# The last block of an attention: its sums by TensorE and VectorE, its store in two parts

## The chip, the cores and the metric

The kernel runs on one core of a Trainium2 chip. The metric is the device time of one execution in microseconds (us), as the median of several runs. The core's engines are TensorE (PE; its weight loads are PEld), VectorE (DVE), ScalarE (ACT), GpSimd (POOL) and SyncE (SP), which here only issues transfers. Each engine works through its own list in order, and they wait for one another by semaphores.

## The reference, cut to what matters

Two images of 32 channels and 64 x 64 positions go through four layers, each added to its input; the last is an attention over all N = 4096 positions of an image.

```python
def _L3_conv_ref(x, w1, b1, w2, b2, w3, b3):
    xf = x.reshape(Bb, Cc, N)
    f1 = jnp.einsum('oc,bcn->bon', w1, xf) + b1[None, :, None]
    f2 = jnp.einsum('oc,bcn->bon', w2, xf) + b2[None, :, None]
    f3 = jnp.einsum('oc,bcn->bon', w3, xf) + b3[None, :, None]
    A = jax.nn.softmax(jnp.einsum('bcn,bcm->bnm', f1, f2), axis=-1)
    out = jnp.einsum('bcm,bnm->bcn', f3, A) + xf
    return out.reshape(Bb, Cc, Hh, Ww)
...
x = x + _L0_conv_ref(_gn(x), ...)
x = x + _L1_conv_ref(_gn(x), ...)
x = x + _L2_conv_ref(_gn(x), ...)
x = x + _L3_conv_ref(_gn(x), ...)
return x
```

## The kernel before

The attention is done one image after the other, each in eight blocks (`NBLK`) of 512 queries (`BLK`). Within a block a loop `s` goes over eight groups (`KEY_QUADS`) of four tiles of 128 keys. For each `s`:

- TensorE makes the scores of four key tiles, one to a PSUM bank (the banks `SCORES` to `SCORES + 3`), with a second, short product of three rows that subtracts each query's maximum;
- ScalarE takes the exponential of two banks at a time into `probs` (128 keys by 4 x 512 queries, two buffers); `probs_ready` counts the halves;
- TensorE multiplies the probabilities of the group before with the values `f3`. For image 1 (`weigh_values`) the four key tiles go to four column groups of 32, so the bank `SUMS` collects four partial numerators of 32 channels on its 128 partitions;
- for image 1, GpSimd adds the two halves of the probabilities (`add_pair`, 128x1024, into `pair_probs`), and TensorE multiplies the sum with ones (`weigh_ones`): the four column groups take 128 queries each, and the bank `SAMPLES` collects two halves of the softmax's totals, each 128 columns wide.

When a block of image 1 ends, its sums are finished beside the next block. ScalarE copies three pieces out of PSUM (`copy_sums`: `att_halves` and `halves_of_totals`). GpSimd adds the totals (`sum_part` with k = 0) and the numerators' upper and lower 64 partitions (k = 1). VectorE inverts the totals (`invert_totals`). ScalarE moves the second 32 rows of the numerators, and one row out of each of four groups of the inverses, onto image 1's partitions (`move_parts`: `lower_sum`, `inverse_row`). GpSimd adds the two rows of numerators (k = 2), multiplies by the inverse (k = 3) and adds the residual into `x_of[1]` (k = 4). After the last block the same steps run with nothing beside them. For image 0 other code does this on VectorE.

SyncE waits for the semaphore `x_final`, which counts finished blocks of both images, and stores each image whole: 32 partitions of 4096 numbers, 512 KB.

`stack` is a column of three 32x32 identities, used in an earlier layer to add three groups of 32 partitions by one product; VectorE makes it near 275 us by copies from `ident`. The pairs of lines that matter most, at the end of GpSimd's and of VectorE's program:

```python
for k in range(5):
    sum_part((0, 0, NBLK - 1), k, beside=False)
...
invert_totals((0, 0, NBLK - 1))
v.wait_ge(x_final, NBLK * B)
```

Of the kernel before, what the change touches and what calls it, by code (L numbers as in the profile page):

```python
# [67 lines left out]
def build(nc, x, off_w, off_b, conv_w, gamma, beta, l1_w, l1_ax, l1_aw, off2_w, off2_b, conv2_w, conv2_b,  # L68
# [10 lines left out]
    with ctx:  # L79
# [50 lines left out]
        stack = sb("stack", [3 * C, C])  # L130
# [61 lines left out]
        packed_values = scratch[:, 6 * BLK:8 * BLK].rearrange("p (m n) -> p m n", n=P)  # L192
        att_halves = scratch[0:2 * C, 4 * BLK:6 * BLK].rearrange("p (h n) -> p h n", h=2)
# [73 lines left out]
        x_final = sem("x_final"); pairs_added = sem("pairs_added"); parts_moved = sem("sum_parts_moved"); pool_sums = sem("pool_sums")  # L267
# [143 lines left out]
        def _(sp):  # L411
# [77 lines left out]
            for b in range(B):  # L489
                sp.wait_ge(x_final, NBLK * (b + 1))  # L490
                sp.dma_start(out[b].rearrange("c h w -> c (h w)"), x_of[b]).then_inc(out_stored, 16)
            sp.wait_ge(out_stored, 16 * B)

        @block.gpsimd
        def _(pool):
# [147 lines left out]
            def sum_part(j, k, beside=True):  # L643

                if 0 < k < 5 and beside:
                    pool.wait_ge(pairs_added, lin(j, KEY_QUADS, KEY_QUADS + k + 1))
                num, quotient = att_sum[IMAGE[1], 1, :], att_sum[IMAGE[1], 2, :]
                if k == 0:
                    pool.wait_ge(sums_copied, lin(j, 1, NBLK + 1))
                    pool.tensor_tensor(totals, halves_of_totals[:, 0:P], halves_of_totals[:, P:], ALU.add).then_inc(pool_sums, 1)  # L650
                elif k == 1:
                    pool.wait_ge(pool_sums, lin(j, POOL_SUMS, 1))
                    pool.tensor_tensor(att_sum[:, 0, :], att_halves[:, 0, :], att_halves[:, 1, :], ALU.add).then_inc(pool_sums, 1)
                elif k == 2:
                    pool.wait_ge(parts_moved, lin(j, 1, 1))
                    pool.tensor_tensor(num, att_sum[IMAGE[1], 0, :], lower_sum, ALU.add).then_inc(pool_sums, 1)
                elif k == 3:
                    pool.wait_ge(pool_sums, lin(j, POOL_SUMS, 3))
                    pool.tensor_tensor(quotient, num, inverse_row, ALU.mult).then_inc(pool_sums, 1)
                elif k == 4:  # L660
                    pool.wait_ge(pool_sums, lin(j, POOL_SUMS, 4))
                    at = lin(j, BLK)
                    here = slice(at, at + BLK) if isinstance(at, int) else bass.ds(at, BLK)
                    pool.tensor_tensor(x_of[1][:, here], x_of[1][:, here], quotient, ALU.add).then_inc(x_final, 1)

            def await_sum_part(j, k):
# [3 lines left out]
                elif k == 4:  # L670
                    pool.wait_ge(x_final, lin(j, 1, NBLK + 1))

            def second_attention():
# [9 lines left out]
                for s in range(KEY_QUADS):  # L683
# [3 lines left out]
                for k in range(5):  # L687
                    sum_part((0, 0, NBLK - 1), k, beside=False)
# [4 lines left out]
        def _(v):  # L693
# [307 lines left out]
            def place_bands():  # L1001
# [22 lines left out]
                for q in range(3):  # L1024
# [218 lines left out]

            def sum_part(b, j, k):
# [63 lines left out]
            def attention(b):  # L1308
# [10 lines left out]
                else:  # L1319
# [6 lines left out]
                    invert_totals((0, 0, NBLK - 1))  # L1326
                    v.wait_ge(x_final, NBLK * B)
# [70 lines left out]
        def _(act):  # L1398
# [284 lines left out]
            def attention(b):  # L1683
# [7 lines left out]
                else:  # L1691
# [7 lines left out]
                    copy_sums(b, (0, 0, NBLK - 1))  # L1699
                    move_parts((0, 0, NBLK - 1))  # L1700
# [50 lines left out]
        def _(pe):  # L1751
# [190 lines left out]
            def add_parts(i):  # L1942
# [5 lines left out]
                pe.matmul(psum[0:C, ADDED_BANK, 0:w], stack[:, :], conv_parts[:, 0:w], start=True, stop=True).then_inc(parts_added, 1)  # L1948
# [127 lines left out]

            def weigh(b, j, s, half):
# [74 lines left out]
            def attention(b):  # L2152
# [7 lines left out]
                else:  # L2160
# [7 lines left out]
                    weigh_values((0, 0, NBLK - 1), KEY_QUADS - 1)  # L2168
                    weigh_ones((0, 0, NBLK - 1), KEY_QUADS - 1)
# [72 lines left out]
```

## Time and profile before

| | before |
|---|---|
| median of three runs | 1275.58 us |
| lowest and highest of them | 1274.82 and 1275.71 us |
| the profiled execution, its own time | 1271.83 us |
| its span, from the first instruction to the last | 1270.0 us |
| busy in the span: PE, DVE, ACT, POOL | 1147.7, 956.1, 677.8, 684.8 us |
| mean granted TensorE clock, as a share of full speed | 0.948 |

The span is what the views of the trace cover; the execution's own time holds it and what lies around it. The profiled execution is one execution, and is not among the three runs. Busy times are sums over the whole span. They say little on the last 20 us, where one engine works at a time.

### The profile page before, as it was taken

How to read it: one execution, taken by the hardware profiler on the slowest of the kernel's cores; microseconds unless marked ns; L12 is line 12 of the kernel's file. 1: busy time of each engine (PE TensorE's matmuls, PEld its weight loads, DVE VectorE, ACT ScalarE, POOL GpSimd, SP SyncE). 2: the span in 40 equal slices, each digit the busy share in tenths (PEclk: the TensorE clock that was granted, in tenths of full speed). 3: DMA queues.
4: the chain of work that ended last, by engine and by line, in shares of the span. 5: the costliest groups of instructions: out<-in, count | busy, mean ns of one | idle time of the engine just before them, and what ended most of it. 6: DMA issues, size and time to landing. Idle time of an engine off the chain costs nothing.

```text
span 1270.0 us, 21675 instructions
## 1 busy us (share of the span) xinstructions
PE 1147.7 (90%) x7638; PEld 488.2 (38%) x7638; DVE 956.1 (75%) x1631; ACT 677.8 (53%) x930; POOL 684.8 (54%) x641
## 2 busy tenths in 40 slices
PE   4999997688999999979898898889899999999994
PEld 1788885154544443423332322232222222222221
DVE  6699998875766666668878888888768777777740
ACT  4876775756454555322244443443754466666663
POOL 7000000027777777777777777776000367777776
PEclk9999998698999999965699999999999899999998
DMA  2656550048454442111111111111000000000000
GB/s 55 143 130 122 114 118 1 1 141 253 138 145 128 149 143 70 52 48 50 52 53 52 50 52 51 50 52 48 1 1 1 1 18 1 0 1 0 1 1 17
DMA packets 59675, 79.26 MB, mean 62 GB/s; under 512 B 12230, under 2 KB 43974, under 8 KB 59414
## 3 DMA queue, kind: packets, MB, share of 16 engines
q1 hardware_dynamic: 44342, 47.03, 14.5%
q0 software_dynamic: 15264, 31.29, 8.7%
q8 instruction: 46, 0.75, 0.2%
q14 instruction: 23, 0.19, 0.1%
HBM read 70.94 MB, written 7.34 MB: 62 GB/s over the span
## 4 chain that ended last, share of the span: by engine, by line
PE 40%; POOL 34%; issue 14%; DVE 6%; ACT 3%; SPq 1%; DMA 1%; POOLq 0%; DVEq 0%; ACTq 0%
POOL tile_data L565 33%; PE psum L2107 6%; PE psum L2048 6%; PE psum L1813 6%; PE psum L2064 4%; PE psum L1828 3%; PE psum L2084 3%; DVE maxes L1215 2%; PE psum L1840 2%; PE psum L1763 2%; PE psum L2073 1%; PE psum L2113 1%; PE psum L2011 1%; PE psum L1831 1%; ACT quads L1667 1%
## 5 line engine op out<-in xcount | busy, mean ns | idle before, releaser
L565 POOL DMA_INDIRECT tile_data<-quad_table,index_u x477 | 467.0, 979 | 389.5 <-DMA quad_table<-quad_rows_or_splits 244.4
L1215 DVE TENSOR_REDUCE maxes<-psum 128x1 f32<-128x512 f32 x512 | 326.2, 683 | 90.4 <-PE psum L2048 89.0
L1667 ACT ACTIVATE quads<-psum 128x1024 f32<-128x1024 f32 x256 | 248.1, 1021 | 222.0 <-PE psum L2113 221.3
L640 POOL TENSOR_TENSOR tile_data<-quads 128x1024 f32<-128x1024 f32 x64 | 150.5, 2351 | 177.8 <-ACT quads L1667 132.4
L1928 PE MATMUL psum<-scratch,quad_rows_or_splits 128*128 128x512 f32 (+1 forms) x486 | 211.5, 577 | 6.7 <-DVE scratch L1037 6.7
L2107 PE MATMUL psum<-quads,probs_and_weighted 32*128 32x512 f32 x1024 | 147.2, 644 | 2.5 <-ACT quads L1667 2.4
L2084 PE MATMUL psum<-quads 128*64 128x512 f32 x512 | 131.2, 617 | 0.0
L1928 PEld LDWEIGHTS psum<-scratch,quad_rows_or_splits 128*128 128x128 f32 x486 | 88.6, 193 | 104.0 <-issue 88.7
L2048 PE MATMUL psum<-products_or_attention 128*128 128x512 bf16 x256 | 90.5, 416 | 37.0 <-DVE maxes L1215 37.0
L1049 DVE TENSOR_TENSOR probs_and_weighted<-psum,quads 128x512 f32<-128x512 f32 (+1 forms) x81 | 51.4, 642 | 75.9 <-PE psum L1928 70.7
L1512 ACT ACTIVATE vals<-psum 96x384 f32<-96x384 f32 x53 | 25.8, 486 | 142.8 <-PE psum L1892 142.8
L2048 PE MATMUL psum<-quad_rows_or_splits,tile_data 128*128 128x512 bf16 x256 | 82.6, 389 | 5.3 <-DVE maxes L1215 3.6
L1813 PE MATMUL psum<-quad_rows_or_splits 64*128 64x128 f32 x1152 | 81.4, 283 | 1.5 <-DVE in_reach L817 1.5
L1542 ACT ACTIVATE quads<-quads,band_columns 128x512 f32<-128x512 f32 (+1 forms) x81 | 49.6, 676 | 54.8 <-DVE probs_and_weighted L1049 54.8
L2048 PEld LDWEIGHTS psum<-products_or_attention 128*128 (+1 forms) x256 | 19.9, 98 | 149.2 <-DVE maxes L1215 106.3
L1813 PEld LDWEIGHTS psum<-quad_rows_or_splits 64*128 64x128 f32 x1152 | 69.3, 187 | 12.4 <-issue 6.3
L2064 PE MATMUL psum<-quads 128*32 128x512 f32 x512 | 68.2, 605 | 0.8 <-ACT quads L1667 0.7
L952 DVE TENSOR_TENSOR probs_and_weighted<-tile_data,psum 128x1152 f32<-128x1152 f32 x45 | 60.6, 1346 | 0.3
L831 DVE TENSOR_TENSOR probs_and_weighted<-psum,tile_data 128x384 f32<-128x384 f32 x96 | 52.8, 550 | 7.0 <-DVE sampled L850 5.1
L1763 PE MATMUL psum<-quads,off_w 128*32 128x512 f32 x256 | 32.8, 659 | 27.5 <-DMA w_sb<-in_b 17.8
L2107 PEld LDWEIGHTS psum<-quads,probs_and_weighted 32*128 32x128 f32 x1024 | 40.4, 184 | 44.8 <-issue 22.2
L1037 DVE SCALAR_TENSOR_TENSOR scratch<-products_or_attention,band_columns,psum 128x512 f32<-128x512 f32 (+1 forms) x81 | 51.8, 692 | 5.2 <-ACT psum L1547 5.2
(241 smaller groups left out, 1578.7 us busy)
## 6 DMA issues: line engine op xcount, KB each, us to landing
products_or_attention<-positions SPq DMA_DIRECT2D x30, 576.0 KB, 8.4
products_or_attention<-bands SPq DMA_DIRECT2D x12, 768.0 KB, 7.3
tile_data<-quad_table,index_u POOLq DMA_INDIRECT x477, 2.5
quads<-bands SPq DMA_DIRECT2D x6, 768.0 KB, 10.5
quad_table<-quad_rows_or_splits SPq DMA_DIRECT2D x4, 768.0 KB, 8.3
products_or_attention<-bands SPq DMA_DIRECT2D x4, 576.0 KB, 8.5
quad_table<-quad_rows_or_splits SPq DMA_DIRECT2D x2, 640.0 KB, 8.4
products_or_attention<-positions SPq DMA_DIRECT2D x4, 288.0 KB, 6.9
```

Of the source, the lines that this page charges most:

```text
L565: pool.indirect_dma_start(out=out[:, k * CORNERS * C:(k + 1) * CORNERS * C], out_offset=None, in_=table, in_offset=bass.IndirectOffsetOnAx ...
L640: pool.tensor_tensor(pair_probs[:, s % 2, :], probs[:, s % 2, 0:2 * BLK], probs[:, s % 2, 2 * BLK:4 * BLK], ALU.add)\
L952: v.tensor_tensor(weighted[:, :].rearrange("p (q k c) -> p k q c", q=CORNERS, c=C), corners_of.rearrange("p (k q c) -> p k q c", k=TAPS, q ...
L1215: v.reduce_max(maxes[:, tile_of_q, block_of_k:block_of_k + 1], psum[:, FREE + c % 2, :], AXIS_X)\
L1667: act.activation(probs[:, s % 2, 2 * BLK * h:2 * BLK * (h + 1)], psum[:, SCORES + 2 * h:SCORES + 2 * h + 2, :].rearrange("p a n -> p (a n) ...
L1763: pe.matmul(psum[C * g:C * g + C, bank, :].rearrange("p (y x) -> p y x", x=W), off_w_sb[d][:, s, :], grid[:, y:y + 8, sx:sx + W], start=s ...
L1813: last = pe.matmul(psum[:, mix_bank(b, ky), P * kx:P * kx + P], hat_x[rows, n % 2, 3 * ky + kx, :], img_t[rows, (2 * n + ky) * C:(2 * n + ...
L1928: last = pe.matmul(psum[:, m, 0:width(n)], band_img[:, j, 4 * C * m:4 * C * (m + 1)], band_sel[:, n % 2, j, 0:width(n)], start=j == 0, sto ...
L2048: pe.matmul(psum[:, FREE + c % 2, :], qa[b][:, tile_of_q], ka[b][:, lo:lo + BLK], start=True, stop=True).then_inc(chunk_scored, 1)
L2064: pe.matmul(psum[C * i:C * i + C, SUMS, :], f3[1][:, 4 * s + i, 0:C], probs[:, s % 2, BLK * i:BLK * i + BLK], start=s == 0, stop=s == KEY_ ...
L2084: last = pe.matmul(psum[2 * C * h:2 * C * h + 2 * C, SUMS, :], f3[b][:, 4 * s + i, :], probs[:, s % 2, BLK * i:BLK * i + BLK], start=s == ...
L2107: pe.matmul(psum[:, SCORES + i, :], keys[b][mine, P * s:P * s + P], q_now[mine, :], start=True, stop=False)
```

## The change

For the last block of image 1 alone, the sums are finished in another way.

- TensorE multiplies both halves of the last group's probabilities with ones itself (two products of four column groups in place of one on the halves' sum), each before the half's values product. GpSimd's last pair sum and its five last `sum_part` steps go.
- VectorE takes the two halves of the totals from PSUM, adds and inverts them (`last_sums`).
- TensorE spreads the inverses: four products with a row of ones, one for each group of 128 queries, from partitions 0, 32, 64 and 96 into four banks, all onto image 1's 32 partitions. ScalarE copies these into `inverse_row`.
- ScalarE copies the whole bank `SUMS` into `last_block`; TensorE adds its four groups of 32 partitions by one product with `stack`, which has a fourth identity now.
- VectorE multiplies that sum by `inverse_row`, out of PSUM, and adds the residual.
- Finished blocks of image 1 count in a semaphore of their own, `second_final`. Image 1 is stored in two parts: seven blocks (448 KB) when the seventh is finished, and the last block (64 KB) when that is.

```diff
-        stack = sb("stack", [3 * C, C])
+        stack = sb("stack", [P, C])
...
+        last_block = scratch[:, 6 * BLK:7 * BLK]
...
-            for b in range(B):
-                sp.wait_ge(x_final, NBLK * (b + 1))
-                sp.dma_start(out[b].rearrange("c h w -> c (h w)"), x_of[b]).then_inc(out_stored, 16)
-            sp.wait_ge(out_stored, 16 * B)
+            sp.wait_ge(x_final, NBLK)
+            sp.dma_start(out[0].rearrange("c h w -> c (h w)"), x_of[0]).then_inc(out_stored, 16)
+            for blocks, here in ((NBLK - 1, slice(0, N - BLK)), (NBLK, slice(N - BLK, N))):
+                sp.wait_ge(second_final, blocks)
+                sp.dma_start(out[1].rearrange("c h w -> c (h w)")[:, here], x_of[1][:, here]).then_inc(out_stored, 16)
+            sp.wait_ge(out_stored, 48)
...
-                for s in range(KEY_QUADS):
+                for s in range(KEY_QUADS - 1):
                     await_sum_part((0, 0, NBLK - 2), s - 1)
                     add_pair((0, 0, NBLK - 1), s, ahead=False)
                     sum_part((0, 0, NBLK - 2), s)
-                for k in range(5):
-                    sum_part((0, 0, NBLK - 1), k, beside=False)
...
-                for q in range(3):
+                for q in range(4):
                     mine = slice(C * q, C * q + C)
                     last = v.tensor_copy(stack[mine, :], ident[mine, mine])
...
+            def last_sums():
+
+                here = slice(N - BLK, N)
+                quotient = att_sum[IMAGE[1], 2, :]
+                v.wait_ge(last_products, 1)
+                v.wait_ge(second_final, NBLK - 1)
+                v.tensor_copy(halves_of_totals[:, 0:P], psum[:, SAMPLES, 0:P]).then_inc(last_steps, 1)
+                v.wait_ge(last_steps, 1)
+                v.tensor_tensor(totals, psum[:, SAMPLES, P:2 * P], halves_of_totals[:, 0:P], ALU.add).then_inc(last_steps, 1)
+                v.wait_ge(last_steps, 2)
+                v.reciprocal(inverses, totals).then_inc(last_steps, 1)
+                v.wait_ge(last_products, 4)
+                v.wait_ge(last_moved, 2)
+                v.tensor_tensor(quotient, psum[IMAGE[1], FREE + 1, :], inverse_row, ALU.mult).then_inc(last_steps, 1)
+                v.wait_ge(last_steps, 4)
+                v.tensor_tensor(x_of[1][:, here], x_of[1][:, here], quotient, ALU.add).then_inc(second_final, 1)
...
-                    invert_totals((0, 0, NBLK - 1))
-                    v.wait_ge(x_final, NBLK * B)
+                    last_sums()
...
-                    copy_sums(b, (0, 0, NBLK - 1))
-                    move_parts((0, 0, NBLK - 1))
+                    act.wait_ge(last_products, 2)
+                    act.activation(last_block, psum[:, SUMS, :], ACT.Identity).then_inc(last_moved, 1)
+                    act.wait_ge(last_products, 3)
+                    act.wait_ge(second_final, NBLK - 1)
+                    act.activation(inverse_row.rearrange("p (g n) -> p g n", g=4), psum[IMAGE[1], SCORES:SCORES + 4, 0:P], ACT.Identity).then_inc(last_moved, 1)
...
+            def end_last_block():
+
+                s, last = KEY_QUADS - 1, 2 * KEY_QUADS * NBLK * B
+                for half in range(2):
+                    pe.wait_ge(probs_ready, last - 1 + half)
+                    if half == 0:
+                        pe.wait_ge(summed, KEY_QUADS * NBLK * B - 1)
+                    by_query = probs[:, s % 2, 2 * BLK * half:2 * BLK * (half + 1)].rearrange("p (h n) -> p h n", h=2)
+                    for g in range(4):
+                        ones_done = pe.matmul(psum[C * g:C * g + C, SAMPLES, 0:2 * P].rearrange("p (h n) -> p h n", h=2), ones[:, 0:C],
+                                              by_query[:, :, P * g:P * g + P], start=False, stop=half == 1)
+                    if half:
+                        ones_done.then_inc(last_products, 1)
+                    for i in (2 * half, 2 * half + 1):
+                        done = pe.matmul(psum[C * i:C * i + C, SUMS, :], f3[1][:, 4 * s + i, 0:C],
+                                         probs[:, s % 2, BLK * i:BLK * i + BLK], start=False, stop=True)
+                done.then_inc(last_products, 1)
+                pe.wait_ge(last_steps, 3)
+                for g in range(4):
+                    done = pe.matmul(psum[IMAGE[1], SCORES + g, 0:P], ones[C * g:C * g + 1, 0:C], inverses[C * g:C * g + 1, :],
+                                     start=True, stop=True)
+                done.then_inc(last_products, 1)
+                pe.wait_ge(last_moved, 1)
+                pe.matmul(psum[IMAGE[1], FREE + 1, :], stack[:, :], last_block, start=True, stop=True).then_inc(last_products, 1)
...
-                    weigh_values((0, 0, NBLK - 1), KEY_QUADS - 1)
-                    weigh_ones((0, 0, NBLK - 1), KEY_QUADS - 1)
+                    end_last_block()
```

How this stands in the engines' lists is shown at three places. The rows give the line, the operation, output and inputs, the output's shape, and what an instruction waits for. The names are those of the memory that holds a buffer: `quads` holds `probs` and `f3`; `tile_data` holds `pair_probs`, the totals and the inverses; `scratch` holds the numerators and `last_block`.

TensorE, from the last scores of image 1 to its program's end, before:

```order
L2107 MATMUL psum<-quads,probs_and_weighted 128x512 [waits probs_ready]
...
L2064 MATMUL psum<-quads 32x512 [waits probs_ready]
L2064 MATMUL psum<-quads 32x512 x3
L2073 MATMUL psum<-tile_data,ones 32x256 [waits pairs_added]
L2073 MATMUL psum<-tile_data,ones 32x256 x3
L79 UNCONDITIONAL_BRANCH
```

and with the change, from the seventh group's ones product on:

```order
L2094 MATMUL psum<-tile_data,ones 32x256 x3
L2107 MATMUL psum<-quads,ones 32x256 [waits sums_done,probs_ready]
L2107 MATMUL psum<-quads,ones 32x256 x3
L2112 MATMUL psum<-quads 32x512 x2
L2107 MATMUL psum<-quads,ones 32x256 [waits probs_ready]
L2107 MATMUL psum<-quads,ones 32x256 x3
L2112 MATMUL psum<-quads 32x512 x2
L2117 MATMUL psum<-tile_data,ones 32x128 [waits last_steps]
L2117 MATMUL psum<-tile_data,ones 32x128 x3
L2121 MATMUL psum<-scratch,stack 32x512 [waits last_sums_moved]
L79 UNCONDITIONAL_BRANCH
```

The last wait for GpSimd (`pairs_added`) is gone; two ones products stand ahead of the halves of the values product, and five products on the sums themselves follow, behind waits for VectorE and ScalarE.

VectorE, from the last step on the maxima to its program's end (line 1242 of before is line 1244 of the changed program); before:

```order
L1236 TENSOR_TENSOR nm_parts<-neg_max,nm_parts 128x16 [waits nm_steps]
L1242 RECIPROCAL tile_data<-tile_data 128x128 [waits pool_sums] x2
L79 UNCONDITIONAL_BRANCH [waits x_final]
```

and with the change:

```order
L1244 RECIPROCAL tile_data<-tile_data 128x128 [waits pool_sums]
L1252 COPY tile_data<-psum 128x128 [waits second_image_final,last_products]
L1254 TENSOR_TENSOR tile_data<-psum,tile_data 128x128 [waits last_steps]
L1256 RECIPROCAL tile_data<-tile_data 128x128 [waits last_steps]
L1259 TENSOR_TENSOR scratch<-psum,tile_data 32x512 [waits last_sums_moved,last_products]
L1261 TENSOR_TENSOR x_state<-x_state,scratch 32x512 [waits last_steps]
```

One inverse that waited for GpSimd's totals becomes five operations that wait for TensorE, for ScalarE and for VectorE itself.

GpSimd, from the residual of the seventh block to its program's end, before:

```order
L664 TENSOR_TENSOR x_state<-x_state,scratch 32x512 [waits pool_sums,pairs_added]
L640 TENSOR_TENSOR tile_data<-quads 128x1024 [waits sums_done,probs_ready,x_final]
L640 TENSOR_TENSOR tile_data<-quads 128x1024 [waits sums_done,probs_ready] x2
L650 TENSOR_TENSOR tile_data<-tile_data 128x128 [waits sums_copied]
L653 TENSOR_TENSOR scratch<-scratch 64x512 [waits pool_sums]
L656 TENSOR_TENSOR scratch<-scratch,tile_data 32x512 [waits sum_parts_moved]
L659 TENSOR_TENSOR scratch<-scratch,tile_data 32x512 [waits pool_sums]
L664 TENSOR_TENSOR x_state<-x_state,scratch 32x512 [waits pool_sums]
L79 UNCONDITIONAL_BRANCH
```

and with the change:

```order
L668 TENSOR_TENSOR x_state<-x_state,scratch 32x512 [waits pool_sums,pairs_added]
L644 TENSOR_TENSOR tile_data<-quads 128x1024 [waits sums_done,probs_ready,second_image_final]
L644 TENSOR_TENSOR tile_data<-quads 128x1024 [waits sums_done,probs_ready]
L79 UNCONDITIONAL_BRANCH
```

GpSimd ends with the pair sum of the seventh group; six operations behind it are gone. The rest of all five lists is in the same order as before, apart from the fourth copy into `stack` on VectorE, the three stores at the end of SyncE's list, and ScalarE's two copies in place of eight.

## Rows read from the trace of the kernel before

**Rows 1.** The page's first line: the profiled execution's span.
```profile
span 1270.0 us, 21675 instructions
```

**Rows 2.** Chain that ended last, its end: start us, us, engine and line.
```profile
1253.35 2.36 POOL tile_data L640
...
1264.43 1.29 POOLq L79
```

**Rows 3.** Timeline of the end: start us, us, engine, line, operation, count, idle before.
```profile
1245.57 1.26 POOL L664 TENSOR_TENSOR x_state<-x_state,scratch 32x512 f32<-32x512 f32 x1
...
1251.34 1.94 ACT L1667 ACTIVATE quads<-psum 128x1024 f32<-128x1024 f32 x2 [1.80 <-PE psum L2113]
...
1252.06 0.61 PE L2073 MATMUL psum<-tile_data,ones 128*32 128x256 f32 x8
...
1255.76 0.64 PE L2073 MATMUL psum<-tile_data,ones 128*32 128x256 f32 x8 [1.36 <-POOL tile_data L640]
1256.46 0.59 ACT L1639 ACTIVATE scratch<-psum 64x512 f32<-64x512 f32 x1 [3.19 <-PE psum L2073]
...
1258.13 0.45 POOL L650 TENSOR_TENSOR tile_data<-tile_data 128x128 f32<-128x128 f32 x1 [2.43 <-ACT tile_data L1642]
1258.62 0.95 DVE L1242 RECIPROCAL tile_data<-tile_data 128x128 f32<-128x128 f32 x1 [26.55 <-POOL tile_data L650]
...
1259.95 0.63 ACT L1648 ACTIVATE tile_data<-scratch 32x512 f32<-32x512 f32 x1 [1.90 <-POOL scratch L653]
...
1264.47 1.25 POOL L664 TENSOR_TENSOR x_state<-x_state,scratch 32x512 f32<-32x512 f32 x1
1265.75 0.34 SPq L491 DMA_DIRECT2D out_x<-x_state  x1
```

**Rows 4.** DMA issues: tensors, queue, count, KB each, median us to landing.
```profile
positions<-scratch SPq DMA_DIRECT2D x4, 256.0 KB, 2.0
out_x<-x_state SPq DMA_DIRECT2D x2, 512.0 KB, 3.9
```

**Rows 5.** Windows around both stores: stretch, its length, busy, PEclk, DMA share, GB/s.
```profile
25.40:26.30 0.90, 0.90 (x12) 0.24 (x8) 0.90 (x1) 0.90 (x1) 0.75 (x2) 1.00 0.77 291
...
1265.75:1266.55 0.80, 0.00 (x0) 0.00 (x0) 0.00 (x0) 0.00 (x0) 0.00 (x0) 0.50 0.00 0
1266.55:1269.25 2.70, 0.00 (x0) 0.00 (x0) 0.00 (x0) 0.00 (x0) 0.00 (x0) 0.50 0.92 194
```

**Rows 6.** Timeline, four places: products of the new shapes' nearest kinds on TensorE.
```profile
546.01 1.04 PE L1948 MATMUL psum<-scratch,stack 96*32 96x512 f32 x2 [0.70 <-ACT scratch L1556]
...
700.40 0.84 PE L1900 MATMUL psum<-vals,conv_w 96*32 96x128 f32 x6
...
703.00 1.94 PE L2084 MATMUL psum<-quads 128*64 128x512 f32 x8
...
1249.89 1.14 PE L2107 MATMUL psum<-quads,probs_and_weighted 32*128 32x512 f32 x8
```

**Rows 7.** Groups by line and shape on VectorE: busy us, mean ns, idle before.
```profile
L1049 DVE TENSOR_TENSOR probs_and_weighted<-psum,quads 128x512 f32<-128x512 f32 x54 | 37.1, 688 | 59.2 <-PE psum L1928 55.9 <-PE psum L1938 3.4
L1049 DVE TENSOR_TENSOR probs_and_weighted<-psum,quads 128x384 f32<-128x384 f32 x27 | 14.4, 550 | 16.6 <-PE psum L1928 14.8 <-PE psum L1938 1.8
L1266 DVE TENSOR_TENSOR x_state<-x_state,scratch 32x512 f32 x5 | 3.4, 680 | 0.0
```

**Rows 8.** Timeline: VectorE's next operation behind the copies into `stack`.
```profile
277.67 0.46 DVE L739 COPY scratch<-psum 128x288 f32<-128x288 f32 x1 [2.43 <-PE psum L1871]
```

**Rows 9.** Windows at the end, as in rows 5.
```profile
1253.00:1257.00 4.00, 1.70 (x16) 0.32 (x16) 0.00 (x0) 0.81 (x2) 2.35 (x1) 1.00 0.00 0
1257.00:1260.00 3.00, 0.00 (x0) 0.00 (x0) 0.95 (x1) 1.08 (x4) 1.71 (x2) 1.00 0.00 0
1260.00:1270.00 10.00, 0.00 (x0) 0.00 (x0) 0.00 (x0) 1.70 (x5) 3.76 (x3) 0.51 0.25 52
```

**Rows 10.** DMA queues of 1230 to 1270 us: packets, MB, share of 16 engines.
```profile
q8 instruction: 2, 0.03, 0.4%
```

More of the change, by code:

```diff
@@ L266, in build @@
         sums_copied = sem("sums_copied"); sum_steps = sem("sum_steps"); residuals = sem("residuals_added")
-        x_final = sem("x_final"); pairs_added = sem("pairs_added"); parts_moved = sem("sum_parts_moved"); pool_sums = sem("pool_sums")
+        x_final = sem("x_final"); second_final = sem("second_image_final")
+        last_products = sem("last_products"); last_moved = sem("last_sums_moved"); last_steps = sem("last_steps"); pairs_added = sem("pairs_added"); parts_moved = sem("sum_parts_moved"); pool_sums = sem("pool_sums")
         block = ctx.enter_context(nc.Block())
@@ L641, in add_pair, with sum_part @@
                     .then_inc(pairs_added, 1)
-            def sum_part(j, k, beside=True):
-                if 0 < k < 5 and beside:
+            def sum_part(j, k):
+                if 0 < k < 5:
                     pool.wait_ge(pairs_added, lin(j, KEY_QUADS, KEY_QUADS + k + 1))
@@ L663, in sum_part @@
                     here = slice(at, at + BLK) if isinstance(at, int) else bass.ds(at, BLK)
-                    pool.tensor_tensor(x_of[1][:, here], x_of[1][:, here], quotient, ALU.add).then_inc(x_final, 1)
+                    pool.tensor_tensor(x_of[1][:, here], x_of[1][:, here], quotient, ALU.add).then_inc(second_final, 1)
             def await_sum_part(j, k):
@@ L670, in await_sum_part @@
                 elif k == 4:
-                    pool.wait_ge(x_final, lin(j, 1, NBLK + 1))
+                    pool.wait_ge(second_final, lin(j, 1, 1))
             def second_attention():
@@ L1947, in add_parts @@
                 w = width(TAPS * i)
-                pe.matmul(psum[0:C, ADDED_BANK, 0:w], stack[:, :], conv_parts[:, 0:w], start=True, stop=True).then_inc(parts_added, 1)
+                pe.matmul(psum[0:C, ADDED_BANK, 0:w], stack[0:3 * C, :], conv_parts[:, 0:w], start=True, stop=True).then_inc(parts_added, 1)
             def dense_and_tiles():
```

## Prediction

> **What bounds the kernel now.** I read the page first, for the span: 1270.0 us [rows 1]; the profiled execution took 1271.83 us as a whole, so 1.83 us lie around the span, and the median of the runs, 1275.58 us, is 3.75 us above that execution. I work out the change of the span, and carry it unchanged to the median.
>
> The change touches only what comes after the last block's scores, so the view that matters is the chain of waits at its end [rows 2]: after VectorE's and TensorE's work in the blocks, the last pieces, five of them, are all POOL's, from the pair sum at 1253.35 to 1264.43 and its program's end, with the residual in it. The timeline of that stretch [rows 3] shows why: from the end of the seventh ones product (1252.06 + 0.61 = 1252.67) to the issue of image 1's store at 1265.75 the engines take turns, each waiting for the one ahead. The second exponential of the last group of keys ends at 1251.34 + 1.94 = 1253.28; POOL's pair sum holds the last ones product back until 1255.76; ScalarE moves three pieces from 1256.46; POOL adds the totals from 1258.13, VectorE inverts them in 0.95, POOL adds the parts, ScalarE moves five pieces from 1259.95 on, and POOL does three more operations, the last in 1.25 from 1264.47, until 1265.72. Nothing else is in progress, so each microsecond taken out here is one of the span. The store then lands 3.9 us after its issue [rows 4]. Cut into stretches [rows 5], this is 0.80 us without a byte, 2.70 us of transfer at 194 GB/s, and about 0.4 us more to the landing.
>
> **The change, part by part.** *Removed from the chain:* POOL's last pair sum and its five operations, ScalarE's eight small activations, VectorE's old inverse. The path from 1252.67 to 1265.75, 13.08 us, is replaced.
>
> *Added:* I follow the new path from 1252.67. For each hand-over between engines I take 0.05 us: the rows show 0.06 from TensorE to ScalarE (1255.76 + 0.64 = 1256.40, then 1256.46) and 0.04 from POOL to VectorE (1258.13 + 0.45 = 1258.58, then 1258.62) [rows 3]; I take the same where VectorE waits for itself.
> 1. TensorE starts on the first half of the last probabilities 0.06 after 1252.67, since they are there by then (the second half too, at 1253.28). A ones product over four column groups with 256 columns took 0.64 [rows 3]. There are two instead of one, since the halves are no longer added first. Half of a values product uses two of four column groups; the nearest row is image 0's, with two groups and 512 columns, two halves in 1.94, so 0.97 each [rows 6]. Up to the end of the second ones product: 0.64 + 0.97 + 0.64 = 2.25. The other half of the values (0.97) and ScalarE's copy of the sums (0.59, as at 1256.46) end at about 1256.6, while VectorE works.
> 2. VectorE copies half the totals out of PSUM, adds the other half, inverts. With a PSUM operand it took 688 ns for 512 columns and 550 for 384 [rows 7], 138 less per 128 columns, so 0.27 for 128; I take 0.29, and 0.95 for the inverse: 1.53.
> 3. TensorE spreads the inverses: four products of one row by 128 columns, on four row groups, into four banks. This is not in the trace. One after the other, as three accumulating products of 128 columns took 0.84 [rows 6], it would be 1.12. Side by side, 0.35 at least: one such product is 0.28. The row of the scores, four row groups into four banks, took 1.14 for 512 columns, hardly more than the 1.04 of a single product of 512 columns [rows 6], so row groups do run side by side here; I take 0.45.
> 4. TensorE adds the four column groups by one product with four stacked identities: 1.04, the row of the same product with three [rows 6]. ScalarE's copy of the spread inverses (0.63) is hidden under it.
> 5. VectorE multiplies (0.69, a PSUM operand) and adds the residual (0.68) [rows 7]; then SP issues the store, 0.03 later as now.
>
> Work 2.25 + 1.53 + 0.45 + 1.04 + 1.37 = 6.64; hand-overs 0.06 at the start, six of 0.05, 0.03 at the end: 0.39. The store is issued at 1252.67 + 7.03 = 1259.70, 6.05 earlier.
>
> *The store:* 64 KB in runs of 2 KB instead of 512 KB. The store of positions, 256 KB, landed in 2.0 [rows 4], moving at 291 GB/s [rows 5]; 64 KB take 0.23 at that rate. With 0.80 ahead and 0.3 to 0.4 behind, 1.45; 2.0 is the upper bound, since four times the bytes need no more. Gain 2.45. The rows split that duration into a part which no smaller store loses (1.1 to 1.2) and one that goes with the bytes.
> The Trainium skill, page "DMA: Bandwidth & Descriptors", section "Anatomy of one DMA — SWDGE (gpsimd) path", gives about 2.0 us fixed and 436 GB/s for the rest. By that the small store would take an estimated 2.15, the gain here would be 1.75 and the sum 7.80 instead of 8.50. The trace does not bear it out: the same rule gives 2.6 for the 256 KB that landed in 2.0.
>
> *Moved:* the other 448 KB are issued when block 6 is final, at 1245.57 + 1.26 = 1246.83 [rows 3], and even at the 3.9 us of the whole store have landed some 10 us before the new end; SP has nothing else queued. They run beside block 7, whose POOL operations are on the path; I price that at nothing, as the transfers go to DMA engines that carried nothing there, and at 0.5 at most for two pair sums.
>
> *The fourth identity block* costs VectorE one more 32x32 copy, about 0.17, near 275 us. Behind the copies VectorE waits 2.43 us for TensorE [rows 8], which covers it; bare, it would be 0.2 us.
>
> Sum: 6.05 + 2.45 = 8.50. Span 1261.5, profiled execution 1263.3, median 1267.1.
>
> **The rivals.**
> *The store is no faster when small.* Its time would be a wait for the memory, not the bytes: 3.9 stays, gain 6.05, time 1269.5. For it: the parts before and behind the transfer are constant. Against it: 256 KB in 2.0 and a transfer of 2.70 in the middle of this very store.
> *TensorE's tail is slow.* The granted clock is full (2.4 GHz) over 1253 to 1257 and 1257 to 1260, though TensorE did nothing in the latter; over 1260 to 1270 it is 0.51 [rows 9], half (1.2 GHz) for nearly all of it. If it fell before 1257, steps 3 and 4 would cost 1.49 more; with step 3 one by one, 0.67 more. Time 1267.8 to 1269.3. Against it: the new path keeps TensorE busy to about 1256 and again until 1258, where now it stops at 1256.40.
> *Nothing to measure.* About 0.2%, 2.6 us, is what a measurement of this kernel can tell from no change. The gain would have to shrink by 6 us over seven hand-overs, 0.9 each where the rows show 0.04 to 0.08. Time around 1274.
> *Slower.* Code is fetched by DMA: two packets of the instruction queue in the last 40 us, at 0.4% of sixteen engines' time 1.28 us each [rows 10]. The additional copy near 275 us moves all later code of VectorE, loops included, by one instruction. If a border of what is fetched then fell into a loop, each pass could wait about 1.3 us; from nine such passes (2.6 + 8.5 = 11.1 us) the kernel is slower, with sixteen about 1279. Against it: in the rows of the end no engine waits for code, although such a packet lies among them.
>
> **How the numbers follow.** The forecast has 0.78, the unshortened store 0.08, a slow TensorE 0.07, nothing 0.03, slower 0.04. Within the forecast: step 3 up to 0.67 more or 0.10 less; the store up to 0.55 more; the early part of the store up to 0.5; step 1 about 0.3 less if its pieces overlap. That is 1266.5 to 1268.9, and the runs of before spread over 0.9, so 1266.0 to 1269.3; taking in the rivals that still gain 6 us or more, 1265.3 to 1270.0. Faster by over 0.2%: 0.78 + 0.08 + 0.07 = 0.93; within it 0.03; slower 0.04.
>
> **What would show it.** Right: the timeline of after has the first half's ones product right behind the seventh one's end; VectorE's three small operations in about 1.6; the spreads in under 0.5 with starts close together; the stack product in about 1.04 at full clock; the store issued some 7.0 us after the seventh ones product, and landed about 1.5 after its issue. Wrong: spreads 0.28 apart, a stack product of 2 us, a second store that lands after 2 us or more, VectorE's operations with waits of half a microsecond between them, or a block 7 longer than now while the first part of the store moves.

## The result, and the profile after

The changed kernel took 1265.89 us (median of four runs, 1263.46 to 1266.97) against 1275.20 for before (four runs, 1274.17 to 1275.71). The ratio is 0.9932, with a 95% interval of 0.9917 to 0.9946. The forecast was 1267.1, a ratio of 0.9933. The measured median lies inside the forecast's wide range (1265.3 to 1270.0) and 0.1 us below its narrower one (1266.0 to 1269.3). The profiled execution took 1263.46 us over a span of 1261.7; before it was 1270.0 [rows 1].

The timeline of the changed kernel's end, in the columns of [rows 3], from the residual of block 6 (the seventh, counted from 0) over the seventh ones product, from whose end both kernels' tails are measured, to the issue of the last store (weight loads and some products are left out; L668 is the residual, L2094 the seventh ones product, L2107 are ones products, L2112 values, L2117 spreads, L2121 the stack product):

```profile
1245.85 1.26 POOL L668 TENSOR_TENSOR x_state<-x_state,scratch 32x512 f32<-32x512 f32 x1
...
1252.34 0.61 PE L2094 MATMUL psum<-tile_data,ones 128*32 128x256 f32 x8
...
1253.13 0.64 PE L2107 MATMUL psum<-quads,ones 128*32 128x256 f32 x8 [0.18 <-PE psum L2094]
...
1253.56 0.62 PE L2112 MATMUL psum<-quads 128*32 128x512 f32 x2
1253.62 0.62 PE L2107 MATMUL psum<-quads,ones 128*32 128x256 f32 x4
...
1254.63 0.41 PE L2107 MATMUL psum<-quads,ones 128*32 128x256 f32 x2
1255.12 0.29 DVE L1252 COPY tile_data<-psum 128x128 f32<-128x128 f32 x1 [22.76 <-PE psum L2112]
1255.18 0.60 ACT L1718 ACTIVATE scratch<-psum 128x512 f32<-128x512 f32 x1 [1.63 <-PE psum L2112]
1255.44 0.29 DVE L1254 TENSOR_TENSOR tile_data<-psum,tile_data 128x128 f32<-128x128 f32 x1
1255.77 0.95 DVE L1256 RECIPROCAL tile_data<-tile_data 128x128 f32<-128x128 f32 x1
...
1256.78 0.42 PE L2117 MATMUL psum<-tile_data,ones 1*32 1x128 f32 x8 [1.68 <-DVE tile_data L1256]
...
1257.13 1.06 PE L2121 MATMUL psum<-scratch,stack 128*32 128x512 f32 x2
1257.26 0.59 ACT L1721 ACTIVATE tile_data<-psum 32x512 f32<-32x512 f32 x1 [1.49 <-PE psum L2117]
1258.22 0.68 DVE L1259 TENSOR_TENSOR scratch<-psum,tile_data 32x512 f32<-32x512 f32 x1 [1.50 <-PE psum L2121]
1258.94 0.68 DVE L1261 TENSOR_TENSOR x_state<-x_state,scratch 32x512 f32<-32x512 f32 x1
...
1259.65 0.31 SPq L495 DMA_DIRECT2D out_x<-x_state  x1
```

The seventh ones product ends at 1252.95 here (1252.67 before), the last store is issued at 1259.65: 6.70 us instead of 13.08. Two things are to be seen besides. Values products (from 1253.56) and ones products (from 1253.62) run beside one another, and the last ones product ends at 1254.63 + 0.41 = 1255.04. VectorE's copy at 1255.12 waits, by the program, for that last ones product; the row puts its wait down to the values' line.

Image 1's two stores in the DMA issues of the changed kernel, as in [rows 4]:

```profile
out_x<-x_state SPq DMA_DIRECT2D x1, 448.0 KB, 3.5
out_x<-x_state SPq DMA_DIRECT2D x1, 64.0 KB, 1.6
```

The last store lands in 1.6 us instead of 3.9. The stretch from the seventh ones product to the last landing is so 6.70 + 1.6 = 8.30 instead of 13.08 + 3.9 = 16.98, 8.68 less. The spans differ by 8.3, mostly because the seventh ones product ended 0.28 later in this execution.

### The profile page after: what moved, and what is told of

The parts are those of the page before. It is cut to its first block, busy times and chain, and to the rows that moved or that the text cites. A ratio compares the mean times of both kernels' runs of the same rounds, so it can differ in the third digit from the quotient of the medians.

```text
span 1261.7 us, 21645 instructions
## 1 busy us (share of the span) xinstructions
PE 1139.2 (90%) x7595; PEld 490.1 (39%) x7656; DVE 958.5 (76%) x1636; ACT 675.6 (54%) x924; POOL 678.4 (54%) x635
## 4 chain that ended last, share of the span: by engine, by line
PE 48%; POOL 19%; DVE 14%; issue 12%; ACT 4%; SPq 1%; DMA 1%; DVEq 1%; POOLq 0%; ACTq 0%
POOL tile_data L569 19%; PE psum L2153 8%; PE psum L2069 8%; PE psum L1834 6%; PE psum L2130 5%; DVE maxes L1217 5%; PE psum L2085 4%; PE psum L1849 3%; DVE probs_and_weighted L954 3%; PE psum L1784 2%; PE psum L1861 2%; PE psum L2159 2%; DVE probs_and_weighted L964 2%; PE psum L2094 1%; PE psum L2032 1%
## 5 line engine op out<-in xcount | busy, mean ns | idle before, releaser
L2069 PE MATMUL psum<-products_or_attention 128*128 128x512 bf16 x226 | 83.2, 416 | 42.7 <-DVE maxes L1217 37.6
L2069 PE MATMUL psum<-quad_rows_or_splits,tile_data 128*128 128x512 bf16 x225 | 75.1, 387 | 9.7 <-issue 4.9
```

Source lines behind the costliest of these rows:

```text
L2069: pe.matmul(psum[:, FREE + c % 2, :], qa[b][:, tile_of_q], ka[b][:, lo:lo + BLK], start=True, stop=True).then_inc(chunk_scored, 1)
```

## The experiments

Single executions of one kernel lie some microseconds apart, and the runs here scatter more than those shown first: in the first group before took 1269.87 to 1276.04 in 27 runs, median 1272.77, in the second 1269.15 to 1275.89 in 17, median 1274.18. For steps of one or two microseconds the verdict therefore rests on two stretches of the timeline, each from one profiled execution: from the seventh ones product's end to the last store's issue, and from there to its landing (read to 0.1 us). The first four experiments belong to the first group, the others to the second; the changed kernel was not run in the second, so comparisons with it there go by the stretches.

**The store alone.** The kernel before, with this edit:

```diff
-            for b in range(B):
-                sp.wait_ge(x_final, NBLK * (b + 1))
-                sp.dma_start(out[b].rearrange("c h w -> c (h w)"), x_of[b]).then_inc(out_stored, 16)
+            sp.wait_ge(x_final, NBLK)
+            sp.dma_start(out[0].rearrange("c h w -> c (h w)"), x_of[0]).then_inc(out_stored, 16)
+            for blocks, here in ((2 * NBLK - 1, slice(0, N - BLK)), (2 * NBLK, slice(N - BLK, N))):
+                sp.wait_ge(x_final, blocks)
+                sp.dma_start(out[1].rearrange("c h w -> c (h w)")[:, here], x_of[1][:, here]).then_inc(out_stored, 16)
```

> The kernel before, with only image 1's store in two parts. My theory (the store's gain stands by itself, by the bytes it no longer moves at the end): the last store is issued 13.1 us after the seventh ones product as before, and lands 1.6 us after its issue instead of 3.9, so 2.3 us less, ratio 0.998. Rival A (all of the gain comes from the sums, the split only moves waiting about): within 0.3 us of before. Rival B (the 448 KB beside block 7 take time from GpSimd's pair sums): the gain shrinks to 1.8 us, with pair sums above 2.4 us in the timeline.

Its timeline and its DMA issue of the last store:

```profile
1244.18 1.26 POOL L666 TENSOR_TENSOR x_state<-x_state,scratch 32x512 f32<-32x512 f32 x1
...
1248.21 2.36 POOL L642 TENSOR_TENSOR tile_data<-quads 128x1024 f32<-128x1024 f32 x1 [0.34 <-ACT quads L1669]
...
1250.67 0.61 PE L2075 MATMUL psum<-tile_data,ones 128*32 128x256 f32 x8
...
1264.35 0.31 SPq L493 DMA_DIRECT2D out_x<-x_state  x1
```

```profile
out_x<-x_state SPq DMA_DIRECT2D x1, 64.0 KB, 1.6
```

From 1251.28 to 1264.35 it is 13.07 us, as before, and the store lands in 1.6: up to the landing, 2.3 us are the store's own, as my theory said. The pair sum beside the 448 KB takes 2.36, as elsewhere, and from the end of block 6's residual (1245.44) to the end of the seventh ones product it is 5.84 us, as in before (1246.83 to 1252.67): rival B falls. The ratio of the runs, 0.9992 (0.9980 to 1.0004), cannot tell the expected 0.998 from no change; by itself it leaves rival A open, and the timeline decides.

Not all of the 2.3 us reaches the end of the span in this execution. The span ends 15.62 us after the seventh ones product, against 17.33 in before: 1.7 less. Behind the landing SyncE waits for the end of TensorE's program, here longer than the 0.2 us of the other nine profiles (line, what it waited for, us in total, times, longest):

```profile
SPq L79 <- PEq L79: 0.7, 1, 0.7
```

Why is not known, and one execution does not show whether it returns. What the short store is worth on top of the new sums is seen without it in the next experiment and the changed kernel run once more, in the same group: medians of 1267.00 and 1264.52, and spans that end 10.95 and 8.70 us after the seventh ones product, 2.25 us apart.

**The sums alone.** The changed kernel, image 1 stored whole:

```diff
-            for blocks, here in ((NBLK - 1, slice(0, N - BLK)), (NBLK, slice(N - BLK, N))):
-                sp.wait_ge(second_final, blocks)
-                sp.dma_start(out[1].rearrange("c h w -> c (h w)")[:, here], x_of[1][:, here]).then_inc(out_stored, 16)
+            sp.wait_ge(second_final, NBLK)
+            sp.dma_start(out[1].rearrange("c h w -> c (h w)"), x_of[1]).then_inc(out_stored, 16)
...
```

> The changed kernel, with image 1 stored whole at the end. My theory: the store is issued 6.7 us after the seventh ones product, as in the changed kernel, and lands 3.9 to 4.0 us after its issue; 6.4 us less than before, 2.3 us more than the changed kernel, ratio 0.995. Rival A (all of the gain comes from the sums): 8.7 us less than before.

```profile
1251.84 0.61 PE L2093 MATMUL psum<-tile_data,ones 128*32 128x256 f32 x8
...
1259.14 0.34 SPq L494 DMA_DIRECT2D out_x<-x_state  x1
```

These lines of its timeline give 1259.14 - 1252.45 = 6.69 us; the store of 512 KB lands in 3.9. The ratio is 0.9959 (0.9946 to 0.9972), so 3.6 to 6.9 us, which holds the 6.4 expected and excludes the 8.7 of rival A.

**TensorE's ones alone.** The kernel before without GpSimd's last pair sum; ones and values in the halves' order of the changed kernel, everything behind them as before:

```diff
-                for s in range(KEY_QUADS):
+                for s in range(KEY_QUADS - 1):
                     await_sum_part((0, 0, NBLK - 2), s - 1)
                     add_pair((0, 0, NBLK - 1), s, ahead=False)
...
+            def end_last_block():
...
-                    weigh_values((0, 0, NBLK - 1), KEY_QUADS - 1)
-                    weigh_ones((0, 0, NBLK - 1), KEY_QUADS - 1)
+                    end_last_block()
```

> The kernel before, with only GpSimd's last pair sum replaced by TensorE's two ones products on the halves; copies, totals, parts, quotient, residual and store as before. Theory 1 (the pieces of step 1 overlap over column groups, as the changed kernel's timeline suggests): sums are complete 2.15 us after the seventh ones product instead of 3.73, the store is issued 1.6 us earlier, ratio 0.9988. Theory 2 (the prediction's step 1, durations one after the other: 0.64 + 0.97 + 0.64 + 0.97 and the start): 3.3 us, so 0.4 us earlier. Both: the rest of the chain as long as before.

```profile
1253.18 0.61 PE L2073 MATMUL psum<-tile_data,ones 128*32 128x256 f32 x8
...
1256.00 0.59 ACT L1639 ACTIVATE scratch<-psum 64x512 f32<-64x512 f32 x1 [1.60 <-PE psum L2089]
...
1265.28 0.34 SPq L491 DMA_DIRECT2D out_x<-x_state  x1
```

ScalarE starts 2.21 us after the seventh ones product's end (1253.79), and the store is issued 11.49 after it, 1.59 earlier than before: theory 1, and not a sum of durations as in the prediction's step 1. The ratio, 0.9987 (0.9973 to 1.0001), agrees with 1.6 us, but does not exclude 0.4. So of the 6.4 us of the sums, 1.6 come from the pair sum and, by difference, 4.8 from what follows.

**The changed kernel once more.**

> The changed kernel once more, beside the others. My theory: 8.3 to 9.0 us less than before; the stretch from the seventh ones product's end to the store's issue 6.7 us, the landing 1.6 us. Rival (TensorE's granted clock falls early in some executions, since in the changed kernel's profile it fell at about 1258 us, in the stack product): the stack product takes up to 2.1 us and the stretch 7.7 us.

```profile
1255.29 0.61 PE L2094 MATMUL psum<-tile_data,ones 128*32 128x256 f32 x8
...
1260.09 1.04 PE L2121 MATMUL psum<-scratch,stack 128*32 128x512 f32 x2
...
1262.60 0.32 SPq L495 DMA_DIRECT2D out_x<-x_state  x1
```

1262.60 - 1255.90 = 6.70 again, the landing 1.6, the stack product 1.04 at full clock. The rival's early fall of the clock does not occur in this execution. The ratio is 0.9936 (0.9920 to 0.9952), 8.2 us less, just under the 8.3 to 9.0 expected, all of which the interval holds. Its span, though, is 1264.6, because the seventh ones product ends 3 us later than in the first profile.

**Ones first.** The changed kernel, the ones products of both halves ahead of the values:

```diff
                     for g in range(4):
                         ones_done = pe.matmul(psum[C * g:C * g + C, SAMPLES, 0:2 * P].rearrange("p (h n) -> p h n", h=2), ones[:, 0:C],
                                               by_query[:, :, P * g:P * g + P], start=False, stop=half == 1)
-                    if half:
-                        ones_done.then_inc(last_products, 1)
-                    for i in (2 * half, 2 * half + 1):
-                        done = pe.matmul(psum[C * i:C * i + C, SUMS, :], f3[1][:, 4 * s + i, 0:C],
-                                         probs[:, s % 2, BLK * i:BLK * i + BLK], start=False, stop=True)
+                ones_done.then_inc(last_products, 1)
+                for i in range(4):
+                    done = pe.matmul(psum[C * i:C * i + C, SUMS, :], f3[1][:, 4 * s + i, 0:C],
+                                     probs[:, s % 2, BLK * i:BLK * i + BLK], start=False, stop=True)
```

> The changed kernel, with both of TensorE's ones products on the halves ahead of all four values products. Times from the seventh ones product's end. My theory (the path that ends last goes by the totals; the values have about 1.2 us to spare): VectorE starts at 1.4 us instead of 2.2, the store is issued at 5.9 instead of 6.65, 0.75 us less than the changed kernel. Rival (the values and the stack product end last): VectorE's inverse is earlier, but the store's issue stays within 0.2 us of 6.65.

```profile
1251.47 0.61 PE L2094 MATMUL psum<-tile_data,ones 128*32 128x256 f32 x8
1252.27 1.11 PE L2107 MATMUL psum<-quads,ones 128*32 128x256 f32 x16 [0.18 <-PE psum L2094]
1253.19 1.04 PE L2111 MATMUL psum<-quads 128*32 128x512 f32 x8
1253.44 0.29 DVE L1252 COPY tile_data<-psum 128x128 f32<-128x128 f32 x1 [21.96 <-PE psum L2107]
...
1257.96 0.31 SPq L495 DMA_DIRECT2D out_x<-x_state  x1
```

VectorE starts 1.36 us after 1252.08, and the store is issued after 5.88, 0.82 earlier than in the changed kernel: the totals' path was the longer one. The values, moved behind the ones (L2111), still reach ScalarE in time. The two ones products, one right behind the other on the same four column groups, take 1.11 us and not twice 0.64. The ratio to before is 0.9920 (0.9904 to 0.9937).

**Inverses moved instead of spread.** The changed kernel without the four spreads; ScalarE and VectorE move two rows of inverses each:

```diff
-                pe.wait_ge(last_steps, 3)
-                for g in range(4):
-                    done = pe.matmul(psum[IMAGE[1], SCORES + g, 0:P], ones[C * g:C * g + 1, 0:C], inverses[C * g:C * g + 1, :],
-                                     start=True, stop=True)
-                done.then_inc(last_products, 1)
...
+                v.wait_ge(last_steps, 3)
+                for g in (2, 3):
+                    v.tensor_copy(inverse_row[:, P * g:P * g + P], inverses[C * g:C * g + C, :]).then_inc(last_steps, 1)
...
-                    act.activation(inverse_row.rearrange("p (g n) -> p g n", g=4), psum[IMAGE[1], SCORES:SCORES + 4, 0:P], ACT.Identity).then_inc(last_moved, 1)
+                    for g in range(2):
+                        last = act.activation(inverse_row[:, P * g:P * g + P], inverses[C * g:C * g + C, :], ACT.Identity)
+                    last.then_inc(last_moved, 1)
```

> The changed kernel without the four spreads on TensorE and without ScalarE's copy of them: ScalarE and VectorE move two of the four rows of inverses each, straight to the place where they are multiplied; the stack product no longer stands behind the spreads. My theory (the spreads cost not only their 0.42 us, but hold the stack product back until the inverse is there): the stack product runs from 2.9 to 3.95 us after the seventh ones product's end, beside the inverse, and the store is issued at 5.9 us instead of 6.65. Rival (moves on ScalarE and VectorE are slower than the spreads, as the 1.25 us for four of them before): 1.25 us from the inverse to the product, and no gain over the changed kernel.

```profile
1254.15 0.61 PE L2100 MATMUL psum<-tile_data,ones 128*32 128x256 f32 x8
...
1257.63 1.05 PE L2122 MATMUL psum<-scratch,stack 128*32 128x512 f32 x2 [0.73 <-ACT scratch L1722]
1258.56 0.63 ACT L1726 ACTIVATE tile_data<-tile_data 32x128 f32<-32x128 f32 x2 [0.98 <-DVE tile_data L1256]
1258.56 0.47 DVE L1259 COPY tile_data<-tile_data 32x128 f32<-32x128 f32 x2
1259.32 0.68 DVE L1263 TENSOR_TENSOR scratch<-psum,tile_data 32x512 f32<-32x512 f32 x1 [0.29 <-ACT tile_data L1726]
...
1260.75 0.32 SPq L495 DMA_DIRECT2D out_x<-x_state  x1
```

The stack product now runs beside the inverse (2.87 to 3.92 us after 1254.76), VectorE multiplies 0.71 earlier than in the changed kernel, and the store is issued at 5.99 instead of 6.70. Two moves on each engine take 0.63 and 0.47 side by side; the rival's 1.25 would have been four on one. The ratio is 0.9912 (0.9898 to 0.9927).

**Both of these edits.**

> The changed kernel with both: ones products ahead of the values, and inverses moved by ScalarE and VectorE. My theory: the inverse ends at 3.0 us after the seventh ones product's end, the moves at 3.7, and the stack product, behind the values and ScalarE's copy, at 3.95, so that it ends last; store issued at 5.4 us, 1.25 less than the changed kernel. Rival (the two gains add up): 5.15 us.

```profile
1255.36 0.61 PE L2100 MATMUL psum<-tile_data,ones 128*32 128x256 f32 x8
...
1258.84 1.04 PE L2121 MATMUL psum<-scratch,stack 128*32 128x512 f32 x2 [0.72 <-ACT scratch L1722]
1258.96 0.63 ACT L1726 ACTIVATE tile_data<-tile_data 32x128 f32<-32x128 f32 x2 [0.18 <-DVE tile_data L1256]
...
1259.97 0.68 DVE L1263 TENSOR_TENSOR scratch<-psum,tile_data 32x512 f32<-32x512 f32 x1 [0.54 <-PE psum L2121]
...
1261.40 0.31 SPq L495 DMA_DIRECT2D out_x<-x_state  x1
```

Issued 5.43 us after 1255.97: 1.27 less than the changed kernel, not the 1.53 of both gains added. VectorE's last wait (0.54) is for the stack product: the path through the values, ScalarE's copy and the stack product now ends last. The median, 1261.34, is the lowest of all; the ratio to before, 0.9899 (0.9884 to 0.9915), is 10.8 to 14.8 us, while the two stretches give 13.08 - 5.43 + 2.3 = 9.95. Why the runs show more than the stretches was not settled. The profiled execution, at 1265.22, is the slowest of the five by 3.7 us, and its seventh ones product ends latest of all ten profiles. Between these ten that end, which the edits do not touch, lies up to 4.7 us apart, more than the 2.9 between the medians' difference and the stretches.

**The fourth identity alone.** The kernel before with `range(4)` in place of `range(3)` at the copies into `stack`, and the larger `stack`:

> The kernel before, with only the fourth identity in the stack: one more copy on VectorE near 275 us, so that all of VectorE's later code stands one instruction further. My theory: no difference in the end's stretches (13.1 us from the seventh ones product to the store's issue, landing 3.9 us), and a time within 0.2% of before. Rival (the moved code makes loops wait for code): passes of VectorE's loops longer by about 1.3 us, 2.6 us or more in all.

The ratio is 0.9998 (0.9988 to 1.0008). No cost in VectorE's loops is seen; the interval leaves room for 1.0 us and excludes the rival's 2.6. The end's stretch, however, was 13.42 and not 13.1, by one product:

```profile
1253.58 0.61 PE L2073 MATMUL psum<-tile_data,ones 128*32 128x256 f32 x8
...
1257.27 1.01 PE L2073 MATMUL psum<-tile_data,ones 128*32 128x256 f32 x8 [1.36 <-POOL tile_data L640]
...
1267.61 0.34 SPq L491 DMA_DIRECT2D out_x<-x_state  x1
```

The last ones product took 1.01 us instead of 0.64. The windows of this execution say why; the last three columns are the granted clock, the DMA share and GB/s:

```profile
1253.50:1257.30 3.80, 1.79 (x24) 0.35 (x21) 0.00 (x0) 1.29 (x2) 2.35 (x1) 1.00 0.00 0
1257.40:1258.40 1.00, 0.88 (x8) 0.03 (x4) 0.00 (x0) 0.07 (x1) 0.00 (x0) 0.50 0.00 0
```

The clock had fallen to half (1.2 GHz) after a stretch in which TensorE was busy for 1.79 of 3.80 us. In the profile of before the same products, with TensorE busy for 1.70 of 4.00 us, were followed by full clock until about 1260 [rows 9]; so before's stretch is 13.1 us in two profiles and 13.4 in this one.

## Why the prediction was right, step by step

Forecast and measured, for the profile of the changed kernel:

| step | forecast us | measured us |
|---|---|---|
| start behind the seventh ones product | 0.06 | 0.18 |
| 1: to the second ones product's end | 2.25 | 1.91 |
| 2: hand-over, copy, add, inverse | 1.68 | 1.68 |
| 3: hand-over and spreads, to the stack product's start | 0.50 | 0.41 |
| 4: stack product | 1.04 | 1.06 |
| 5: hand-over, multiply, residual, issue | 1.50 | 1.46 |
| sum | 7.03 | 6.70 |
| landing of the last store | 1.45 | 1.6 |

- The mechanism and both parts of the gain were right, and up to the landing the parts add: 2.3 us by the store alone, 6.4 by the sums alone, 8.7 together. The medians of the runs give 0.9, 5.8 and 8.3, with intervals that hold 2.3, 6.4 and 8.7.
- That the ratio was met to 0.0001 is luck. Its interval is 1.9 us to either side, and the errors of the steps (+0.12, -0.34, -0.09, +0.02, -0.04, and +0.15 at the landing) cancel in part. By its own terms the narrower range should also have been 1266.2 to 1269.3: 1267.1 less 0.4 and plus 1.72 is 1266.7 to 1268.8, where the prediction has 1266.5 to 1268.9.
- Step 1 was mis-sized by 0.34. It added the durations of products that in the rows overlap: values at 1253.56 and ones at 1253.62, which the program puts on different column groups. The run with TensorE's ones alone has the same order and the same shorter time in another surrounding. Different groups are not all of it: two ones products on the same four groups also took 1.11 instead of 1.28 (ones first). The text had named this overlap as 0.3 in its range.
- The start was taken as 0.06, the hand-over from TensorE to ScalarE. Where TensorE waits for its own earlier product, the rows show 0.18.
- Step 3 had the widest bounds, 0.35 to 1.12. The four spreads took 0.42 for all eight records, where one after the other was put at 1.12, so the row groups work side by side here too. Within the sum that was right, but the larger cost of the spreads was not seen: they hold the stack product back until the inverse is there. Without them the kernel issues its store 0.71 earlier.
- The store landed in 1.6 us in all six profiles that have it, and image 1 stored whole in 3.9 in the other four; the forecast from this kernel's own stores was 1.45. In windows of 0.1 us the bytes move from 1260.45 to 1260.85, some 0.4 us, where the prediction took 0.23; the 0.8 ahead of them was right. By the figures of the Trainium skill's page "DMA: Bandwidth & Descriptors", section "Anatomy of one DMA — SWDGE (gpsimd) path", the estimate was 2.15, which this trace does not bear out; the page gives them for transfers on GpSimd's path, and this one is issued by SyncE.
- The early 448 KB cost block 7 nothing: from the end of block 6's residual to the end of the seventh ones product it is 5.84 us without them (before) and with them (1247.11 to 1252.95 here, and the same with the store alone). The fourth copy was covered as said: VectorE's wait behind it went from 2.43 [rows 8] to 2.23, in this line of the changed kernel's timeline:

```profile
278.63 0.46 DVE L741 COPY scratch<-psum 128x288 f32<-128x288 f32 x1 [2.23 <-PE psum L1892]
```

- Of the rivals, an unshortened store is ruled out by the landing, moved code by the run with the fourth identity alone. A slow TensorE was nearer than its 0.07 said: in the changed kernel's profile the clock fell between 1258.0 and 1258.1, with 0.1 to 0.2 us of the stack product left, as its windows show, and the product took 1.06 instead of 1.04. Had it fallen 1 us earlier, the product would by estimate have been 0.6 to 0.9 us longer: at half clock the ones product above went from 0.64 to 1.01, and image 0's values in before's profile from 1.94 [rows 6] to 3.68 (at 992.17 us).

```profile
1253.00:1258.00 5.00, 3.19 (x34) 1.27 (x34) 1.53 (x3) 1.73 (x3) 0.00 (x0) 1.00 0.02 3
1258.10:1259.00 0.90, 0.08 (x1) 0.00 (x0) 0.74 (x2) 0.00 (x0) 0.00 (x0) 0.50 0.00 0
```

## What to carry to other kernels

At the end of a kernel, where engines hand one small piece of work after another along, the pieces on the path that ends last are the price, and a piece taken off it brings its time, up to the point where another path ends last (both edits together gave 1.27 us here, not 1.53). Durations may only be added where the rows do not overlap. Count there, and store early whatever is final early, so that the last store is small. Then ask which of two paths ends last, and order the work for it: here the totals needed their products first, and a product that waited for the inverse stood ahead of one that did not. Steps of one or two microseconds are read from a stretch between two fixed points of the timeline, when single executions lie several microseconds apart.

## What the runs showed of the hardware that was not expected

The end of the seventh ones product lay between 1251.28 and 1255.97 us in these ten profiles, though the code ahead of it is the same but for a copy. A part of that is TensorE's clock where the kernel passes from image 0's attention to image 1's. In the windows of 985 to 1000 us the granted clock was, in the kernel before, in the one with moved inverses and in the one with the sums alone:

```profile
985.00:1000.00 15.00, 13.41 (x72) 3.77 (x68) 7.36 (x17) 7.88 (x11) 2.34 (x1) 0.77 0.01 2
```

```profile
985.00:1000.00 15.00, 13.42 (x72) 4.32 (x72) 8.56 (x19) 7.87 (x10) 2.35 (x1) 0.89 0.01 2
```

```profile
985.00:1000.00 15.00, 13.42 (x90) 4.44 (x88) 9.73 (x20) 8.82 (x12) 2.35 (x1) 1.00 0.01 2
```

The first pair sum of image 1's attention starts at 992.63, 996.09 and 995.31 us in these three. From there to the end of the seventh ones product it is 260.0, 258.7 and 257.1 us: the lower the clock, the longer. Of the other seven profiles, four have full clock in this window and 257.1 or 257.2 us, and two have 0.89 and 258.6 or 258.7. The seventh, the first profile of the changed kernel, has 0.89 and 257.2 us: there the slow stretch, 991.8 to 995.2, had ended when the first pair sum started at 995.77. Of the 4.7 us between the earliest and the latest of the ten ends, 1.5 go with the clock behind that pair sum, and 3.2 lie ahead of it. The fall comes in some executions and not in others, beside the same code; what decides it, these runs do not tell. The other differences, earlier in the kernel, were not traced.
